# An attention and mixture-of-experts layer: second masks and keys on other engines, the first plan ahead of the last x2, four shared half-layers on either side of the pairs

## The chip, the cores and the metric

The kernel runs on one core of a Trainium2 chip. The metric is the time of one execution on the device, in microseconds (us); the table below also has the span, which is the time from the first to the last recorded instruction. Engines are called by the profile's names too: PE is TensorE (PEld its weight loads), DVE is VectorE, ACT is ScalarE, POOL is GpSimd, SP is SyncE. ACTq and SPq are the DMA issues of these engines.

## What is computed

2048 tokens (two sequences of 1024) of width 128 go through one layer. All of it is float32.

```python
# attention: 8 heads of 16, 2 key-value groups, a window of 32, a sink term in the softmax
mask = (j <= i) & (j > i - WIN)
scores = where(mask, q @ k.T / sqrt(HD), FP16_MIN)
m = max(scores.max(-1), sink_bias)
e = exp(scores - m)
attn = e / (e.sum(-1) + exp(sink_bias - m))
x = layernorm(x + attn @ v @ Wo.T + bo)
# feed-forward: one shared expert for all tokens, and the best 2 of 8 experts for each
shared = (silu(x @ sw1) * (x @ sw2)) @ sw3
w, idx = top_k(softmax(x @ rw + rb), 2)        # w is normalised to a sum of 1
routed = sum of w * ((silu(x @ ew1[e]) * (x @ ew2[e])) @ ew3[e]) over the two experts e
x = layernorm(x + shared + routed)
```

## The kernel before

**Attention.** The tokens are worked off in four chunks of 512 (CHUNKS; `last` is 3), each in four sets of 128 queries. Keys lie in kM (two tiles, used in turn), whose lower 64 partitions hold a mask pattern that is multiplied in with the scores. VectorE writes the masks of both tiles (`spread_masks`, L1043; those of the second at L1448) and the first chunk's keys (L1058); ScalarE writes the keys of the later chunks (`keys`, L846). Per set: scores (PE L581), maximum (DVE L1072), shift (L1079), exp (ACT L872), transposes, weighing of the values (PE L597), `normalise` (DVE L1090 to L1096). Per chunk: `turn` (L1104), the output projection, the sum with x and its statistics (L1106 to L1119), the reciprocal root (POOL L1556), and x2, the normalised rows (DVE L1129; for the last chunk ACT L894).

**Routing.** For every chunk x2 is transposed (PE L619), the router's scores are made (L626), `logits` (DVE L1133) finds the best two experts, `rank` (PE L630) counts places, `gates` and `places` (DVE) give a gate and a row number (pos) for each pick, and `keep_ends` stores how far each expert's list has grown. GpSimd then scatters the chunk's rows into x_list in HBM, eight indirect DMAs of 128 rows each (L1582). The lists are cut into tiles of 128 rows by plans that VectorE works out: the first part (8 tiles) from the counts of chunks 0 and 1 (`plan_full`, `plan_first`), the second (8 tiles) with those of chunk 2, the third (23 tiles) with those of chunk 3. A plan ends with a table (L1219) of row numbers and experts, from which SP, PE, ACT and DVE read registers. `fill_ends` (SP L472) writes eight blocks of blank rows behind the lists' ends; it waits for fill_done, which `keep_ends(last)` gives.

**Experts.** The tiles are taken in 20 pairs (one has a single tile). The iterations of the last stage are numbered by i, and all engines run through them in the same order: iterations 0 to 4 (FIRST_SHARED = 5) are halves of the shared expert's layer for a chunk ("shared half-layers", two for each chunk), 5 to 24 are the pairs, 25 to 27 the last three half-layers. An iteration is: ups (PE L680 and L684, or L694 for a pair), silu (ACT L913, L916), h (DVE L1335, L1339), and, one or two iterations later, downs (PE L711, L725). A pair also needs its rows loaded (SP L483) and turned (PE L667, ACT L907), and its experts' weights copied (DVE L1349, ACT L934). ACT scales its result into y (L925), and POOL scatters y into z_rows in HBM, one indirect DMA for each tile (L1590), 39 in all.

**End.** SP loads z_rows back in five pieces of rows (L488), each when the pairs that can hold its tokens are scattered. VectorE adds shared part and results, makes the statistics, ScalarE and VectorE scale, and SP stores four blocks of rows (L492).

**What sets the order.** Each engine's program is written out by hand and is worked off in order; semaphores tie them together. So POOL never begins with results before the last chunk's scatters, and SP's loads, fills and stores stand in one queue. The order of the steps in iterations 0 to 8 is given by the `if i == ...` lines in the three loops over i (PE L798, ACT L1009, DVE L1498). The names of chunk 2's steps there are written `last - 1`. A few lines of POOL's and SP's programs:

```python
for n in range(CHUNKS - 1):
    scatter(n, 0, 2)
    rstd1_of(n + 1)
    scatter(n, 2)
scatter(last)
for pair in range(ALL_PAIRS):
    scatter_results(pair)
rstd2_of_first()
add_last_results()
```

## Time and profile before

| | |
|---|---|
| time, median of 3 runs | 162.68 us (162.44 to 164.52) |
| time of the profiled execution | 162.66 us |
| its span | 160.6 us |
| busy: PE, DVE, ACT, POOL | 141.4, 117.9, 109.0, 91.1 us |
| mean granted clock of TensorE | 0.979 |

Busy times overlap each other; an engine can be busy for 57% of the span and still be waited for in a part of it. The rows further down are from one profiled execution. A timeline row gives start, length and the instruction with output<-input, and in brackets how long its engine was idle before it and what released it. "issue" there means that it waited for nothing that the profile shows. All starts are counted from the span's start.

### The profile page before, as it was taken

The page shows a single profiled execution, that of the slowest core. Times are in us where ns is not written, and L with a number is a line of the kernel's source. Part 1 is how long each engine was busy: PE and PEld are TensorE (multiplying, and loading weights), DVE is VectorE, ACT ScalarE, POOL GpSimd, SP SyncE. Part 2 cuts the span into 40 slices and gives each one's busy share as a digit, 9 for nine tenths or more (in the row PEclk, how much of TensorE's full clock was granted, in tenths as well). Part 3 has the DMA queues.
Part 4 walks back from the last instruction along what each step waited for, and adds up shares of the span by engine and source line. Part 5 has one row for each costly group of instructions (what it writes and reads, how often), then busy time and mean ns, then how long its engine had stood idle before and what let it go on. Part 6 is the DMA issues. An engine that isn't in the chain of part 4 may idle for free.

```text
span 160.6 us, 3700 instructions
## 1 busy us (share of the span) xinstructions
PE 141.4 (88%) x1078; PEld 119.7 (75%) x1078; DVE 117.9 (73%) x412; ACT 109.0 (68%) x230; POOL 91.1 (57%) x99
## 2 busy tenths in 40 slices
PE   6977978999999889999799999999999999999300
PEld 2166748689959877855479999999999999966300
DVE  6769976998999999999879569234243356786781
ACT  3495999899799986622834567667676676544770
POOL 8723600300284745578777777777776666778430
PEclk9999999999999999999999999999999999999965
DMA  4499960000000110011351753466531191060444
GB/s 83 108 309 379 420 265 6 0 2 0 4 33 33 52 37 17 33 50 50 88 136 50 168 155 99 115 152 171 133 83 49 33 291 52 20 162 10 131 129 132
DMA packets 16962, 17.01 MB, mean 106 GB/s; under 512 B 2555, under 2 KB 15361, under 8 KB 16816
## 3 DMA queue, kind: packets, MB, share of 16 engines
q1 hardware_dynamic: 14304, 12.46, 27.3%
q0 software_dynamic: 2272, 4.24, 8.1%
q8 instruction: 9, 0.15, 0.4%
q10 hardware_dynamic: 368, 0.09, 0.3%
q14 instruction: 9, 0.07, 0.2%
HBM read 10.90 MB, written 6.33 MB: 107 GB/s over the span
## 4 chain that ended last, share of the span: by engine, by line
PE 52%; DVE 18%; ACT 10%; issue 10%; POOL 5%; DMA 2%; ACTq 0%; SPq 0%; DVEq 0%; POOLq 0%
PE att L694 11%; PE gu L694 11%; PE q_bank L725 6%; PE att L725 5%; PE att L581 3%; POOL x_list L1582 3%; PE att L667 3%; ACT probT L884 3%; DMA xT<-x_cols 2%; DVE prob L1079 2%; DVE mx L1072 2%; PE post L626 2%; PE q_bank L556 2%; ACT prob L872 2%; ACT qT L834 2%
## 5 line engine op out<-in xcount | busy, mean ns | idle before, releaser
L1590 POOL DMA_INDIRECT z_rows<-y,xin x39 | 38.9, 996 | 14.1 <-issue 13.5
L1582 POOL DMA_INDIRECT x_list<-x,pos x32 | 31.7, 989 | 25.0 <-DVE x L1162 11.2
L694 PE MATMUL att<-xt,w_pair 128*128 128x128 f32 x160 | 19.6, 275 | 0.0
L694 PEld LDWEIGHTS att<-xt,w_pair 128*128 128x128 f32 x160 | 18.7, 192 | 0.0
L581 PE MATMUL att<-kM,qT 96*128 96x128 f32 x128 | 15.7, 277 | 3.3 <-ACT kM L849 1.6
L694 PE MATMUL gu<-xt,w_pair 128*128 128x128 f32 x152 | 18.6, 275 | 0.0
L597 PEld LDWEIGHTS att<-vbd,probT 128*128 128x128 f32 x128 | 15.4, 191 | 3.4 <-DVE vbd L1065 1.6
L581 PEld LDWEIGHTS att<-kM,qT 96*128 96x128 f32 x128 | 14.8, 192 | 4.0 <-issue 4.0
L694 PEld LDWEIGHTS gu<-xt,w_pair 128*128 128x128 f32 x152 | 17.8, 192 | 0.0
L597 PE MATMUL att<-vbd,probT 128*128 128x128 f32 x128 | 16.8, 280 | 0.5 <-ACT probT L884 0.5
L1339 DVE TENSOR_TENSOR h<-sil,att 128x512 f32<-128x512 f32 x10 | 6.9, 686 | 14.1 <-ACT sil L916 12.2
L1339 DVE TENSOR_TENSOR h<-sil,gu 128x512 f32<-128x512 f32 (+1 forms) x10 | 6.6, 658 | 11.1 <-ACT sil L916 11.1
L872 ACT ACTIVATE prob<-prob 128x512 f32<-128x512 f32 x16 | 10.1, 629 | 4.3 <-DVE prob L1079 4.1
L866 ACT ACTIVATE vT<-gu,bias 32x512 f32<-32x512 f32 x16 | 12.3, 772 | 0.4
L1072 DVE TENSOR_REDUCE mx<-att 128x8 f32<-128x512 f32 x16 | 10.8, 673 | 2.4 <-PE att L581 2.4
L1079 DVE SCALAR_TENSOR_TENSOR prob<-mx,sink,att 128x512 f32<-128x512 f32 x16 | 11.8, 740 | 0.4
L934 ACT ACTIVATE w_pair<-w 128x512 f32 x19 | 11.9, 628 | 0.1
L588 PE MATMUL att<-cst,prob 128*128 128x128 f32 x64 | 9.7, 279 | 1.9 <-ACT prob L872 1.6
L588 PEld LDWEIGHTS att<-cst,prob 128*128 128x128 f32 x64 | 7.2, 140 | 5.5 <-ACT prob L872 4.3
L834 ACT ACTIVATE qT<-q_bank,bias 32x512 f32<-32x512 f32 x15 | 10.2, 679 | 1.2 <-PE q_bank L556 0.9
L916 ACT ACTIVATE sil<-att 128x512 f32<-128x512 f32 x10 | 6.0, 597 | 7.0 <-PE att L694 7.0
L725 PE MATMUL q_bank<-w,h 128*128 x80 | 10.6, 275 | 0.0
(190 smaller groups left out, 305.4 us busy)
## 6 DMA issues: line engine op xcount, KB each, us to landing
w<-weights SPq DMA_DIRECT2D x1, 3456.0 KB, 15.3
xin<-x_list SPq DMA_DIRECT2D x39, 65.0 KB, 2.2
z<-z_rows SPq DMA_DIRECT2D x3, 512.0 KB, 4.6
z_rows<-y,xin POOLq DMA_INDIRECT x39, 2.3
x_list<-blank SPq DMA_DIRECT2D x9, 65.0 KB, 4.0
xT<-x_cols SPq DMA_DIRECT2D x2, 256.0 KB, 3.9
xr<-x_rows SPq DMA_DIRECT2D x2, 256.0 KB, 4.6
xT<-x_cols SPq DMA_DIRECT2D x1, 512.0 KB, 6.6
```

Source lines behind the costliest of these rows:

```text
L581: mm = pe.matmul(att[s][:, j * P:(j + 1) * P], qT[:, s * BPG + j, :, :], kM[n % 2][:, :, at:at + 2 * QB], start=True, stop=True)
L588: mm = pe.transpose(att[s][:, j * P:(j + 1) * P], prob[:, s, j * P:(j + 1) * P], ident)
L597: mm = pe.matmul(att[s][:, j * P:(j + 1) * P], probT[:, s % 2, j * P:(j + 1) * P], vbd[:, at:at + P], start=True, stop=True)
L694: mm = pe.matmul(gu_of(i, q)[:, c * P:(c + 1) * P], w_pair[:, pair % 2, q, c * P:(c + 1) * P], xt[:, pair % 2, q * P:(q + 1) * P], start=T ...
L725: mm = pe.matmul(into[:, q * D:(q + 1) * D], h[:, i % RING, cols], w[:, bass.ds(at[q] + (DOWN + k * D), D)], start=q == 0 and k == 0, stop ...
L834: act.activation(qT[0:GD, :, i, :], blocks(q_bank[rows, :], QB), ACT.Identity, bias=bias[rows, B_Q:B_Q + 1]).then_inc(q_sb, 1)
L872: act.activation(prob[:, s, :], prob[:, s, :], ACT.Exp, scale=-SCALE).then_inc(exp_done, 1)
L1072: dve.tensor_reduce(mx[:, s, :], att[s][:, :].rearrange(by_row, k=2 * QB), AX.X, ALU.max).then_inc(max_done, 1)
L1079: dve.scalar_tensor_tensor(prob[:, s, :].rearrange(by_row, k=2 * QB), mx[:, s, :].unsqueeze(2).to_broadcast([P, BPG * GROUPS, 2 * QB]), si ...
L1339: dve.tensor_tensor(blocks(h[:, i % RING, 0:n * HIDDEN], HIDDEN), blocks(sil[:, i % 2, 0:n * HIDDEN], HIDDEN), blocks(turns[i % 2][:, 0:n ...
L1582: pool.indirect_dma_start(x_list[:, :], bass.IndirectOffsetOnAxis(ap=pos[:, n, k, j:j + 1], axis=0), x2[:, n * ROWT + j, k * ROWW:(k + 1) ...
L1590: pool.indirect_dma_start(z_rows[:, :], bass.IndirectOffsetOnAxis(ap=xin[:, r, q, R_ID:R_ID + 1].bitcast(U32), axis=0), y[:, r, q, :], Non ...
```

## The change

- The masks of the second key tile are written by GpSimd (two copies ahead of its bias sums), and chunk 1's keys by VectorE, between its normalisations of sets 1 and 2 of chunk 0. PE waits for the new semaphore.
- FIRST_SHARED is 4: iterations 0 to 3 are shared, 4 to 23 are the pairs, 24 to 27 are shared.
- On VectorE `plan_first` moves from iteration 1 to 0, and the last chunk's `add_x` and `statistics1` from 0 to 1. The last chunk's transposes, router and rank on PE move from iterations 3, 4 and 4 to 4, 5 and 6 and stand behind the ups there; ScalarE's and VectorE's steps of that chain follow (x2T_out to 5, tanh to 6, logits to 5, gates, places and ends to 6).
- `fill_ends` stands ahead of the loads of pairs 6 and 7 (it stood behind the loads of pair 7).
- y is counted by tile instead of by pair, so that GpSimd can scatter a pair's first tile before the second is scaled.
- Rows of z_rows are numbered so that a piece's load reads one run for each partition.
- At the end the square roots of tiles 8 to 12 come ahead of the first scales, the scales are grouped differently, and the store of tiles 8 to 12 is issued by ScalarE.

The core of the diff:

```diff
-FIRST_SHARED = 5
+FIRST_SHARED = 4
 R_END = FIRST_SHARED + ALL_PAIRS
...
 XRING = 12
+
+PIECES = [(0, 4), (4, 8), (8, 12), (12, 14), (14, 16)]
...
+        def tiles_of(pairs):
+
+            return pairs + second_tiles(pairs)
+
         def tile_weights(eng, engines, pair, q):
...
                 sp.dma_start(z[:, r0:r1, :, :], z_rows[2 * P * r0:2 * P * r1, :]
-                             .rearrange("(t p k) d -> p t k d", p=P, k=2)).then_inc(z_in[piece], 16)
+                             .rearrange("(p t k) d -> p t k d", p=P, k=2)).then_inc(z_in[piece], 16)
...
             for g in range(len(PARTS)):
-                if g == 2:
-                    fill_ends()
                 sp.wait_ge(table_done, g + 1)
...
                 for pair in range(FIRST_PAIR[g], FIRST_PAIR[g + 1]):
+                    if pair == FIRST_PAIR[1] + 2:
+                        fill_ends()
                     load_rows(pair, row)
...
             store_result(0, 8)
-            sp.wait_ge(scaled, 12)
-            store_result(8, 12)
             sp.wait_ge(result_done, 2)
...
                     if n == 1:
-                        pe.wait_ge(masks_done, 5)
+                        pe.wait_ge(later_masks_done, 2)
                     after(pe, k_sb, GROUPS * n)
...
                     pe.wait_ge(base_done, pair + 1)
-                after(pe, y_done, pair - 1)
+                after(pe, y_done, tiles_of(pair - 1) if pair > 1 else 0)
                 into = y_banks[pair % 2]
...
                         rank(last - 1)
-                    if i == 4:
-                        route(last)
                     ups_shared(i, *shared_of(i))
...
                     turn_rows(0)
+                if i == FIRST_SHARED:
+                    transpose_x2(last)
+                if i == FIRST_SHARED + 1:
+                    route(last)
+                if i == FIRST_SHARED + 2:
+                    rank(last)
                 if shared_of(i - 2) is not None:
                     down_shared(i - 2, *shared_of(i - 2))
-                if i == 3:
-                    transpose_x2(last)
-                if i == 4:
-                    rank(last)
                 if pair_of(i - 1) is not None:
...
                 for q in range(width(pair)):
-                    ins = act.activation(y[:, r, q, :], y_banks[pair % 2][:, q * D:(q + 1) * D], ACT.Copy,
-                                         scale=xin[:, r, q, R_GATE:R_GATE + 1])
-                ins.then_inc(y_done, 1)
+                    act.activation(y[:, r, q, :], y_banks[pair % 2][:, q * D:(q + 1) * D], ACT.Copy,
+                                   scale=xin[:, r, q, R_GATE:R_GATE + 1]).then_inc(y_done, 1)
...
             queries(1, 3, HPG)
-            keys(1, 0)
-            keys(1, 1)
             values(1)
...
                     rows_turned(pair_of(i + 1))
-                if i == 4:
+                if i == FIRST_SHARED + 1:
                     x2T_out(last)
+                if i == FIRST_SHARED + 2:
                     router_tanh(last)
...
             act.activation(warm[:, :], eps[:, 0:ROWT], ACT.Sqrt)
+            deviations(8, 12, 3)
             act.wait_ge(first_shift2_done, 1)
-            scale2(0, 4)
-            deviations(8, 12, 3)
-            scale2(4, 8)
+            scale2(0, 8)
             deviations(12, 14, 4)
             act.wait_ge(shift2_done, 1)
-            scale2(8, 10)
+            scale2(8, 9)
             deviations(14, 16, 5)
-            scale2(10, 12)
+            scale2(9, 12)
+            act.wait_ge(scaled, 12)
+            act.dma_start(out[8 * P:12 * P, :].rearrange("(t p) d -> p t d", p=P), total[:, 8:12, :]).then_inc(stored, 16)
...
-            def spread_masks(i):
+            def spread_masks():
                 for at in (GD, GD + QB):
-                    dve.tensor_copy(kM[i][at:at + QB, :, :].rearrange("p g (b k) -> p (g b) k", k=2 * QB),
+                    dve.tensor_copy(kM[0][at:at + QB, :, :].rearrange("p g (b k) -> p (g b) k", k=2 * QB),
                                     pattern[at:at + QB, :].unsqueeze(1)
...
                                       ALU.add).then_inc(q_sb0, 1)
-                dve.wait_ge(kv_mm, 1)
+                keys(0, k_sb0)
+
+            def keys(n, done):
+                dve.wait_ge(kv_mm, n + 1)
                 for g in range(GROUPS):
-                    dve.tensor_scalar(kM[0][0:GD, g, QB:QB + CT], kv_bank[0:GD, :],
+                    dve.tensor_scalar(kM[n][0:GD, g, QB:QB + CT], kv_bank[0:GD, :],
                                       bias[0:GD, B_KVS + g:B_KVS + g + 1], bias[0:GD, B_KVB + g:B_KVB + g + 1],
-                                      ALU.mult, ALU.add).then_inc(k_sb0, 1)
+                                      ALU.mult, ALU.add).then_inc(done, 1)
...
             dve.wait_ge(mask_in, 16)
-            spread_masks(0)
+            spread_masks()
             dve.wait_ge(masks_done, 2)
...
                 softmax_shift(0, s)
-            spread_masks(1)
             dve.wait_ge(place_in, 16)
...
                 normalise(n, 1)
-                if n > 0:
+                if n == 0:
+                    keys(1, k_sb)
+                else:
                     logits(n - 1)
...
                     keep_ends(2)
+                    plan_first()
+                if i == 1:
                     add_x(last)
                     statistics1(last)
-                if i == 1:
-                    plan_first()
                 if i == 2:
...
                 if i == 3:
-                    logits(last)
-                if i == 4:
-                    gates(last)
-                    places(last)
-                    keep_ends(last)
                     add_shared(0)
...
                     add_shared(1)
+                    logits(last)
+                if i == 6:
+                    gates(last)
+                    places(last)
+                    keep_ends(last)
                 if i == 7:
...
+            def spread_later_masks():
+                pool.wait_ge(mask_in, 16)
+                for i in range(2):
+                    at = GD + i * QB
+                    pool.tensor_copy(kM[1][at:at + QB, :, :].rearrange("p g (b k) -> p (g b) k", k=2 * QB),
+                                     pattern[at:at + QB, :].unsqueeze(1)
+                                     .to_broadcast([QB, GROUPS * KW // (2 * QB), 2 * QB])).then_inc(later_masks_done, 1)
+                    pool.wait_ge(later_masks_done, i + 1)
+
             def add_bias(n):
...
                 r = pair % XRING
-                pool.wait_ge(y_done, pair + 1)
                 for q in range(width(pair)):
+                    pool.wait_ge(y_done, tiles_of(pair) + q + 1)
                     pool.indirect_dma_start(
...
             pool.wait_ge(odd_picks_done, 1)
+            spread_later_masks()
             for n in range(CHUNKS):
...
     c[0, C_BASE:C_BASE + EXPERTS] = begin
-    token = np.arange(CHUNKS * ROWT)[None, :, None] * P + row[:, None, None]
-    c[:, C_PLACE:C_PLACE + 2 * CHUNKS * ROWT] = (2 * token + np.arange(2)).reshape(P, -1)
+
+    place = np.zeros((P, CHUNKS * ROWT, 2), np.float32)
+    for r0, r1 in PIECES:
+        place[:, r0:r1] = (2 * P * r0 + 2 * (r1 - r0) * row[:, None, None]
+                           + np.arange(2 * (r1 - r0)).reshape(1, r1 - r0, 2))
+    c[:, C_PLACE:C_PLACE + 2 * CHUNKS * ROWT] = place.reshape(P, -1)
     c[:, C_NOWHERE] = NOWHERE + row
...
     left = np.arange(LEFT)
```

The three places at which the order matters most. First VectorE in iterations 0 to 2, before; `h` rows (L1335) are the ends of iterations, L1109 to L1123 are the last chunk's sum and statistics, L1199 to L1248 the first plan, of which the middle is left out here:

```order
L1181 COPY ends<-post 32x8
L1109 TENSOR_TENSOR res<-att,xr 128x512
L1115 BN_STATS bn<-res 128x6 x4
L1119 BN_AGGR mv<-bn 128x2 x4
L1123 TENSOR_SCALAR lowered<-mv 128x4
L1335 TENSOR_TENSOR h<-sil,att 128x512
L1199 TENSOR_SCALAR passed<-reach,num 32x8
L1201 TENSOR_TENSOR hop<-passed,skip 32x8
```

The same place now (L1204 begins the plan, L1340 is h):

```order
L1250 TENSOR_SCALAR capped<-reach 32x8
L1253 TENSOR_TENSOR since<-capped 32x8
L1340 TENSOR_TENSOR h<-sil,att 128x512
L1114 TENSOR_TENSOR res<-att,xr 128x512
L1120 BN_STATS bn<-res 128x6 x4
L1124 BN_AGGR mv<-bn 128x2 x4
L1128 TENSOR_SCALAR lowered<-mv 128x4
L1340 TENSOR_TENSOR h<-sil,gu 128x512
```

The plan and the second h have moved ahead of the statistics. Next VectorE at the last chunk's places, before: pick and picked are the end of logits, the next h is that of the last shared iteration ahead of the pairs, and pos follows it:

```order
L1151 TENSOR_TENSOR pick<-cst,topi 128x64
L1156 TENSOR_TENSOR picked<-pick 128x32
L1335 TENSOR_TENSOR h<-sil,gu 128x512
L432 TENSOR_LOAD table
L1349 ISA
L1349 COPY w_pair<-w 128x512
L1162 TENSOR_SCALAR x<-half 128x4 x2
L1168 TENSOR_TENSOR placed<-pick,post 128x64
L1173 TENSOR_REDUCE pos<-placed 128x8
L1180 CAST table<-post 1x8
```

The same place now; here the h is that of iteration 6, the third pair (L1344 instead of L1340):

```order
L1156 TENSOR_TENSOR pick<-cst,topi 128x64
L1161 TENSOR_TENSOR picked<-pick 128x32
L1344 TENSOR_TENSOR h<-sil,gu 128x512
L439 TENSOR_LOAD table
L1354 ISA
L1354 COPY w_pair<-w 128x512
L1167 TENSOR_SCALAR x<-half 128x4 x2
L1173 TENSOR_TENSOR placed<-pick,post 128x64
L1178 TENSOR_REDUCE pos<-placed 128x8
L1185 CAST table<-post 1x8
```

The chain up to pos reads the same, but it now ends in iteration 6. Last PE from the last free down to the first pair, before; the transposes (L619) and the router (L626) stand ahead of the pairs:

```order
L711 MATMUL q_bank<-w,h 128x128 x4
L619 MATMUL post<-cst,x 128x128 x4
L680 MATMUL gu<-x2T,w 128x512
L626 MATMUL post<-pw,x2T 128x128 x4
L684 MATMUL gu<-x2T,w 128x512
L654 TENSOR_LOAD table
L667 MATMUL att<-cst,xin 128x128 x2
```

And now, where the transposes (L622) follow the first pair's ups (L697) and the router (L629) the second's:

```order
L714 MATMUL q_bank<-w,h 128x128 x4
L657 TENSOR_LOAD table
L670 MATMUL att<-cst,xin 128x128 x2
L697 MATMUL gu<-xt,w_pair 128x128 x8
L622 MATMUL post<-cst,x 128x128 x4
L714 MATMUL att<-w,h 128x128 x4
L657 TENSOR_LOAD table
L670 MATMUL att<-cst,xin 128x128 x2
L697 MATMUL att<-xt,w_pair 128x128 x8
L629 MATMUL post<-pw,x2T 128x128 x4
```

One shared half-layer has gone from there to the end, and the last chunk's routing has gone in between the pairs.

## Rows read from the trace of the kernel before

**Rows 1.** The page's part 4, shares of the chain that ended last, by engine.

```profile
PE 52%; DVE 18%; ACT 10%; issue 10%; POOL 5%; DMA 2%; ACTq 0%; SPq 0%; DVEq 0%; POOLq 0%
```

**Rows 2.** Timeline of POOL, last chunk's scatters and results; columns: start, length, instruction [idle before].

```profile
84.78 0.96 POOL L1582 DMA_INDIRECT x_list<-x,pos  x1 [0.51 <-DVE pos L1173]
...
95.06 1.00 POOL L1590 DMA_INDIRECT z_rows<-y,xin  x1 [0.30 <-issue]
...
119.75 0.98 POOL L1590 DMA_INDIRECT z_rows<-y,xin  x1 [0.30 <-issue]
...
146.72 0.98 POOL L1590 DMA_INDIRECT z_rows<-y,xin  x1 [0.30 <-issue]
```

**Rows 3.** The tail: timelines of SP and DVE, and the loads of z by tile.

```profile
149.17 0.87 SPq L488 DMA_DIRECT2D z<-z_rows  x2
...
DMA to landing us min/median/max: 2.9/3.9/5.6
...
152.55 0.42 DVE L1362 TENSOR_TENSOR acc<-base,z 128x256 f32<-128x256 f32 x1
...
156.74 1.49 SPq L492 DMA_DIRECT2D out<-total  x3
```

**Rows 4.** Timeline from the start to chunk 1's first maximum.

```profile
5.63 1.44 POOL L1629 COPY qT<-cst 32x1024 f32<-32x1024 f32 x1
...
8.16 1.52 DVE L1058 TENSOR_SCALAR kM<-gu,bias 32x512 f32<-32x512 f32 x2 [0.17 <-PE gu L564]
...
17.33 2.64 DVE L1045 COPY kM<-pattern 32x1152 f32<-32x1152 f32 x2
...
19.93 1.07 PE L564 MATMUL gu<-xT,pw 128*64 128x512 f32 x2
...
22.20 0.16 DVE L1090 SCALAR_TENSOR_TENSOR den<-esink,att 128x8 f32<-128x8 f32 x1 [0.48 <-PE att L597]
...
23.88 0.71 DVE L1104 STREAM_TRANSPOSE oT<-o 128x512 f32<-128x512 f32 x1
...
24.61 2.02 PE L581 MATMUL att<-kM,qT 96*128 96x128 f32 x16 [1.60 <-ACT kM L849]
...
25.78 0.69 DVE L1072 TENSOR_REDUCE mx<-att 128x8 f32<-128x512 f32 x1 [1.18 <-PE att L581]
```

**Rows 5.** Timeline of the routing stage: statistics, plan, x2, loads, pos, fills.

```profile
73.21 0.38 DVE L1119 BATCH_NORM_AGGREGATE mv<-bn 128x2 f32<-128x6 f32 x4
...
74.35 0.22 DVE L1199 TENSOR_SCALAR passed<-reach,num 32x8 f32<-32x8 f32 x1
...
76.28 2.08 ACT L894 ACTIVATE x<-res,shift,rstd 128x256 f32<-128x256 f32 x4 [1.87 <-POOL shift L1561]
...
84.17 0.22 DVE L1173 TENSOR_REDUCE pos<-placed 128x8 uint32<-128x64 f32 x1
...
92.04 4.97 SPq L475 DMA_DIRECT2D x_list<-blank  x8
```

**Rows 6.** Timeline and chain: the first pair's ups, their silu, and the pieces of an iteration.

```profile
84.06 2.01 PE L694 MATMUL att<-xt,w_pair 128*128 128x128 f32 x16
...
86.10 0.60 ACT L916 ACTIVATE sil<-att 128x512 f32<-128x512 f32 x1 [1.46 <-PE att L694]
...
86.07 0.89 PE att L711 x8
86.96 0.22 PE att L667 x2
87.18 1.79 PE gu L694 x16
```

**Rows 7.** Stretches of 1 us at the end: busy time by engine, granted clock, DMA share, GB/s.

```profile
150.00:151.00 1.00, 0.08 (x1) 0.00 (x0) 0.96 (x7) 0.61 (x2) 0.28 (x2) 1.00 0.45 113
...
153.00:154.00 1.00, 0.00 (x0) 0.00 (x0) 0.96 (x2) 0.76 (x2) 0.92 (x2) 0.85 0.00 0
154.00:155.00 1.00, 0.00 (x0) 0.00 (x0) 0.96 (x6) 0.31 (x2) 0.43 (x1) 0.50 0.29 78
```

2 lines of the change are left out of this document (1 added, 1 removed).

## The prediction

> **What bounds the kernel now.** I read first the page's chain of work. It gives PE 52% of the span [rows 1], and it looks as if TensorE set the end all through. The chain is followed back from the last instruction, though, and an engine that is late without being named is found only in its own timeline. So I read GpSimd's timeline next [rows 2]. GpSimd works through one fixed row: for each of the four chunks eight scatters into x_list, then 39 scatters of results into z_rows. The reader is to see three things there. The last chunk's scatters start at 84.78, 0.51 us after GpSimd came free, released by pos: it had just run out of work. From then on it is back to back: eight scatters from 84.78 to 95.06 (10.28 us), and result scatters at a pace of (119.75 - 95.06) / 19 = 1.30 us. At that pace the 38 steps to the last scatter would take 49.4 us, and they take 51.66 (95.06 to 146.72). So its whole slack between pos and the last scatter, time in which it waits for results, is 2.3 us. The last scatter starts at 146.72, and the loads of the last z pieces are issued 2.45 us later, at 149.17. They land 2.9 us after that at the least, and VectorE's last sums start at 152.55 [rows 3]. From there to the end of the span are 8.05 us. So the end hangs on GpSimd's scatters as much as on TensorE, and what starts them is pos of the last chunk.
>
> **The second masks and keys.** VectorE spends 17.33 to 19.97 on the second kM's masks, and then is the last to be ready for chunk 1 [rows 4]. Without them it normalises sets 0 and 1 while TensorE still works. The second K and V projection ends at 19.93 + 1.07 = 21.0. VectorE's two key instructions take as long as the first two, 1.52, so to 22.6. The two last normalisations took 22.20 to 23.88, with a wait in it that is over by then: 1.3, to 23.9. The turn takes 0.71, to 24.6. The first maximum of chunk 1 starts there and not at 25.78, after 1.18 us of idling: 1.2 us gained, and everything behind moves up by it. ScalarE loses its two key instructions, so it isn't late either. The bounds: 1.7 if only TensorE's scores counted, and 0 if GpSimd's two copies disturb the start. They cost about 1.44 x 1152 / 1024 = 1.6 us each, from 7.1 to 10.3, ahead of the bias sums, which wait for a load until 10.9 anyway; beside them stand VectorE's first keys at 8.16. I take 1.2.
>
> The Trainium skill, "SBUF — State Buffer", says on the port pair that VectorE and GpSimd share (section "SBUF: two separate sides") that it is an exclusive lock, held for a whole instruction, so that the loser fully blocks; on VectorE's side it counts fast-mode operations and those with two SBUF inputs. If VectorE's first keys were among them, they would wait out a mask copy of 1.6 us, and the gain of 1.2 would be a loss of 0.4. They have one input, from PSUM, so by the page's own list they aren't. No row here settles it.
>
> **The first plan ahead of the last x2.** All times from here on are on the clock of the profiled execution; the 1.2 comes off at the end. The plan of the first part runs from 74.35, and until then VectorE first did the sum and the statistics of chunk 3, done at 73.21 + 0.38 = 73.59 [rows 5]. Now the plan (1.8) and the second h (0.67) stand ahead of them: 76.1, 2.5 us later. The first table is 2.7 us earlier. GpSimd's reciprocal roots and ScalarE's x2 follow the statistics: x2 runs from 76.28 + 1.5 = 77.8 (it waited 1.87 before, and ScalarE has nothing else meanwhile) to 79.85. Only then come ScalarE's weight copy and the last silu ahead of the pairs (both 128x512, 0.6 by the silu in [rows 6]) and the first turned rows (half as wide, 0.4), to 81.4. So TensorE, with one shared half-layer less ahead, turns the first rows (loaded earlier, with the table) and does its last free down by about 78.2, stands idle and starts the first pair's ups at 81.7 instead of 84.1 [rows 6]. Of the 2.6 us of the moved half-layer some 2.4 are won there.
>
> **Where pos of the last chunk goes.** Before, logits, gates and places of the last chunk are done in iterations 3 and 4, both shared; pos ends at 84.17 + 0.22 = 84.4 [rows 5]. Now the transposes stand behind the ups of iteration 4, the router behind those of 5, rank behind those of 6, and these three are pairs. By the pieces of [rows 6] (ups 1.8, a down 0.9, turned rows 0.2): iteration 4 is ups 81.7 to 83.5, transposes 0.5, down 0.9: 84.9. Iteration 5: rows and ups to 86.9, router 0.9, two downs 1.8: 89.6. Iteration 6: ups from 89.8. Their silu starts 2.0 after them, as in [rows 6], at 91.9, takes 0.6, then h 0.7, a weight copy 0.4, gates 0.25, places and pos 0.45: 94.0. Logits run beside this (from 89.5 to 91.3) and don't add. So pos is 9.6 us later: 94.0, and GpSimd starts at 94.4.
>
> **The sum.** First result scatter: 94.4 + 10.28 = 104.7. At 1.30 each, with results waiting all the way, the last one starts at 104.7 + 49.4 = 154.1, against 146.72: 7.3 later. Loads of z 2.45 later, landing 2.9: 159.4 (before: 152.1, VectorE free at 152.5). Then the tail, 8.05 before. In it SP issues three stores one behind the other, 1.49 us from 156.74 on [rows 3], and the one of tiles 8 to 12 is first. On ScalarE's queue it no longer holds up the two others, which then go out one issue (some 0.45 us) earlier; ScalarE's own store follows its last scale by as much and lands no later. I save 0.45; if ScalarE's store is the last to land, nothing. That z_rows is read in longer runs I count at nothing for its 2.9 (bounds -0.5 and +0.3; it touches no other step), and the counts of y per tile too, since GpSimd is behind by 3 to 10 us all the time and never waits for one. So 159.4 + 7.6 = 167.0; less 1.2 for the attention: 165.8 of span.
>
> To that comes what TensorE does. fill_ends now stands in SP's queue ahead of the loads of pairs 6 and 7, and waits for the last chunk's counts, which come with pos: 94.0. One more us to read the numbers, then the eight fills, 4.97 [rows 5], then the loads: pair 6 is there at about 103, and TensorE wants it at 98.9. Queued behind the fills are all later loads, so TensorE stands still 4 us or more; the loads of pair 8 wait besides for the last chunk's scatters, and come just in time. TensorE then ends at 157.5 and not at 150.1, with the fourth shared half-layer (2.6) behind. VectorE has its shared sums by 158.8, 0.6 ahead of z. That much is cover. But TensorE's granted clock falls when it rests at the end: it comes to rest at 150.1, and the clock is 0.85 in the slice from 153 and 0.50 after it, the lower of its two levels, 1.2 GHz and not 2.4 [rows 7]. The stop ahead of pair 6 may do the same. What work at the lower level costs afterwards no row shows; I set it between 0 and 3 us (one iteration's 2.9 us taking twice as long), less the cover of 0.6. I take a value in the lower half, 0.8, because the clock may also hold. That makes a span of 166.6. The recorded time was 162.66 for a span of 160.6, 2.06 more, and stands at the median (162.68): 168.7 us, 6.0 slower.
>
> **The rivals.** A: the late pos costs nothing, since TensorE alone sets the end, as the page's chain suggests. Then only the 1.2 of the attention and the 0.45 of the stores count: 161.0. For it: PE is busy 88%. Against it: GpSimd has 2.3 us of slack and loses 9.6. It decides from the point at which pos is less than 3.5 us late (the slack and the 1.2); it would take the last chunk's logits to be done during the shared half-layers. B: GpSimd sets the end, but TensorE keeps its clock and z comes in longer runs: 165.8 + 2.06 = 167.9 less up to 0.5, so 167.4. C: the clock falls in the earlier gap too (78.2 to 81.5). Then the iterations ahead of pos run slow, up to 3 us more, and those stand on GpSimd's own path: 168.7 + 2.9 = 171.6. For it: the gap is long; against it: it is shorter than the rest in [rows 7] at the end of which the clock fell. D: the change is faster, since pairs start 2.4 + 1.2 earlier and the fourth half-layer covers the last scatters: 162.7 - 3.6 - 0.45 = 158.6. That was true if pos stayed where it is.
>
> **How the numbers follow.** My forecast (GpSimd late by 6 to 7, some loss on TensorE) 45%; B 22%; C 18%; A 11%; D 4%. A measurement of this kernel can tell about 2%, 3.25 us, from no change. The forecast, B and C are all slower by more; a small part of B (pos at 92 in place of 94) is not. So slower 0.84, same 0.12, faster 0.04. The range takes in B with pos 1.5 earlier (165.3) and C (171.6): 165.0 to 172.0.
>
> **What would show it.** Right: GpSimd idle for 8 us or so ahead of the last chunk's scatters, released by pos near 92.8 (94.0 less 1.2); the first result scatter near 103.5, then no idling to the end; the last z loads issued near 155.3; TensorE idle before the first pair and for 4 us before pair 5's ups, released by an x_list load; chunk 1's first maximum near 24.6. Wrong: a GpSimd that waits for y in the second half, or pos ahead of 88.

## The result, and the profile after

The changed kernel takes 170.78 us (median; 169.99 to 171.34), against 162.67 (162.44 to 164.52) for the kernel before on the same chip: 1.049 times, with an interval of 1.041 to 1.056. It is slower by some 8 us. Ratios and intervals compare fast executions alone: one that is over 1.5% above the fastest of its kernel is left out of them. The profiled execution took 170.56 us, with a span of 168.3 and a mean granted clock of 0.952 (before: 160.6 and 0.979).

The page's chain of work of the changed kernel, shares by engine, as in [rows 1]:

```profile
PE 46%; DVE 25%; issue 10%; ACT 8%; DMA 4%; SPq 3%; POOL 2%; DVEq 0%; ACTq 0%; POOLq 0%
```

It names TensorE first, and GpSimd at 2%, less than before. As before that is one chain of two. GpSimd's timeline, around the last chunk's scatters and at the end, answers to [rows 2]:

```profile
82.92 0.96 POOL L1597 DMA_INDIRECT x_list<-x,pos  x1 [0.30 <-issue]
93.60 0.96 POOL L1597 DMA_INDIRECT x_list<-x,pos  x1 [9.72 <-DVE pos L1178]
...
104.09 1.00 POOL L1605 DMA_INDIRECT z_rows<-y,xin  x1 [0.30 <-issue]
...
153.32 1.12 POOL L1605 DMA_INDIRECT z_rows<-y,xin  x1 [0.30 <-issue]
...
159.93 0.74 POOL L1629 TENSOR_TENSOR acc<-base,z 128x256 f32<-128x256 f32 x1 [3.23 <-DMA z<-z_rows]
```

In brackets stands what the engine waited for. GpSimd is idle for 9.72 us, until pos of the last chunk comes. The first result scatter starts at 104.09 and no longer at 95.06. From there 38 steps in 49.23 us, 1.30 each, without one wait for a result: the last starts 6.6 us later than before.

TensorE's timeline, its two stops and its end (before, the first pair's ups were at 84.06 [rows 6], with no stop in the pairs):

```profile
75.77 0.61 PE L714 MATMUL q_bank<-w,h 128*128 128x128 f32 x4
79.08 0.41 PE L670 MATMUL att<-cst,xin 128*128 128x128 f32 x2 [2.70 <-ACT xt L910]
79.33 2.61 PE L697 MATMUL gu<-xt,w_pair 128*128 128x128 f32 x16
...
102.95 0.69 PE L670 MATMUL att<-cst,xin 128*128 128x128 f32 x2 [4.61 <-DMA xin<-x_list]
103.43 3.62 PE L697 MATMUL att<-xt,w_pair 128*128 128x128 f32 x16
...
156.68 1.95 PE L714 MATMUL att<-w,h 128*128 128x128 f32 x16
```

The pairs start 4.7 us earlier than before, and TensorE ends 8.6 us later (158.63; before 148.03 + 2.05 = 150.08). The ups of a pair take 1.8 to 2.0 us at the full clock. Here the first take 2.61, and those behind the second stop 3.62. The granted clock, in stretches of 1 us (it is the number behind POOL's), shows why:

```profile
80.00:81.00 1.00, 1.00 (x9) 1.00 (x9) 0.97 (x7) 0.00 (x0) 0.70 (x2) 0.78 0.20 67
81.00:82.00 1.00, 1.00 (x7) 1.00 (x7) 0.90 (x7) 0.03 (x1) 0.69 (x2) 0.50 0.12 42
82.00:83.00 1.00, 1.00 (x6) 1.00 (x5) 0.83 (x6) 1.00 (x2) 0.70 (x2) 0.50 0.08 25
...
84.00:85.00 1.00, 1.00 (x11) 1.00 (x10) 0.11 (x1) 0.44 (x2) 0.00 (x0) 1.00 0.20 67
...
101.00:102.00 1.00, 0.00 (x0) 0.00 (x0) 0.29 (x2) 0.00 (x0) 0.70 (x2) 0.52 0.95 204
...
106.00:107.00 1.00, 1.00 (x6) 1.00 (x6) 0.00 (x0) 0.00 (x0) 0.69 (x2) 0.50 0.34 73
...
108.00:109.00 1.00, 1.00 (x11) 1.00 (x10) 0.74 (x2) 0.57 (x3) 0.95 (x1) 1.00 0.75 197
```

It is at 0.50, the lower level (1.2 GHz), behind both stops: some 3 us long behind the first, from 101 to 107.5 around the second. Where TensorE works at that level it is busy all of each microsecond, and does 6 or 7 instructions in it where it does 11 at the full clock.

The timelines of SP and VectorE in the tail, as [rows 3]:

```profile
93.98 4.43 SPq L480 DMA_DIRECT2D x_list<-blank  x8
98.60 11.28 SPq L488 DMA_DIRECT2D xin<-x_list  x13
...
162.66 2.76 SPq L497 DMA_DIRECT2D out<-total  x3
...
159.14 0.66 DVE L1358 TENSOR_TENSOR base<-att,x 128x512 f32<-128x512 f32 x1
...
160.00 0.96 DVE L1367 TENSOR_TENSOR acc<-base,z 128x256 f32<-128x256 f32 x1
```

VectorE's last sums start at 160.00 (before 152.55), 0.07 us behind GpSimd's on the other half of the tiles. VectorE came to them straight from the shared sums, which hung on TensorE's end. GpSimd's had waited for z. So two chains, one through pos and the scatters and one through TensorE's stops, arrive at the end together. The profile alone can't say what either would cost without the other, and the experiments were made for that.

### The profile page after: what moved, and what is told of

The parts are those of the page before. It is cut to its first block, busy times and chain, and to the rows that moved or that the text cites. A ratio compares the mean times of both kernels' runs of the same rounds, so it can differ in the third digit from the quotient of the medians.

```text
span 168.3 us, 3701 instructions
## 1 busy us (share of the span) xinstructions
PE 144.4 (86%) x1078; PEld 123.6 (73%) x1078; DVE 119.0 (71%) x412; ACT 108.0 (64%) x228; POOL 93.0 (55%) x101
## 4 chain that ended last, share of the span: by engine, by line
PE 46%; DVE 25%; issue 10%; ACT 8%; DMA 4%; SPq 3%; POOL 2%; DVEq 0%; ACTq 0%; POOLq 0%
PE att L697 10%; PE gu L697 10%; PE q_bank L728 5%; PE att L728 4%; DVE prob L1084 3%; PE att L670 3%; DVE mx L1077 2%; PE att L600 2%; DMA xin<-x_list 2%; DMA xT<-x_cols 2%; SPq L480 2%; ACT probT L887 2%; PE post L629 2%; DVE kM L1063 2%; PE att L714 1%
## 5 line engine op out<-in xcount | busy, mean ns | idle before, releaser
L1344 DVE TENSOR_TENSOR h<-sil,att 128x512 f32<-128x512 f32 (+1 forms) x10 | 6.6, 661 | 20.7 <-ACT sil L919 20.7
L697 PE MATMUL att<-xt,w_pair 128*128 128x128 f32 x152 | 20.4, 291 | 0.0
L697 PE MATMUL gu<-xt,w_pair 128*128 128x128 f32 x160 | 20.2, 281 | 0.0
L697 PEld LDWEIGHTS att<-xt,w_pair 128*128 128x128 f32 x152 | 19.4, 207 | 0.1
L697 PEld LDWEIGHTS gu<-xt,w_pair 128*128 128x128 f32 x160 | 19.1, 196 | 0.0
L1344 DVE TENSOR_TENSOR h<-sil,gu 128x512 f32<-128x512 f32 x10 | 6.8, 683 | 13.0 <-ACT sil L919 13.0
L670 PE MATMUL att<-cst,xin 128*128 128x128 f32 x39 | 7.9, 284 | 8.3 <-DMA xin<-x_list 5.6
L670 PEld LDWEIGHTS att<-cst,xin 128*128 128x128 f32 x39 | 4.9, 145 | 9.4 <-DMA xin<-x_list 6.6
L910 ACT ACTIVATE xt<-att 128x256 f32<-128x256 f32 (+1 forms) x20 | 7.5, 373 | 5.7 <-PE att L670 5.6
```

Source lines behind the costliest of these rows:

```text
L670: mm = pe.transpose(x_bank[:, i * P:(i + 1) * P], xin[:, r, i, 0:D], ident)
L697: mm = pe.matmul(gu_of(i, q)[:, c * P:(c + 1) * P], w_pair[:, pair % 2, q, c * P:(c + 1) * P], xt[:, pair % 2, q * P:(q + 1) * P], start=T ...
L1344: dve.tensor_tensor(blocks(h[:, i % RING, 0:n * HIDDEN], HIDDEN), blocks(sil[:, i % 2, 0:n * HIDDEN], HIDDEN), blocks(turns[i % 2][:, 0:n ...
```

## The experiments

All times are beside the kernel before on the same chip (162.67 to 162.72 in the three groups). "Five ahead" means FIRST_SHARED = 5.

**1. The fills back behind pair 7.**

```
-                    if pair == FIRST_PAIR[1] + 2:
-                        fill_ends()
+                if g == 2:
+                    fill_ends()
```

> The changed kernel with fill_ends at its old place, behind the loads of pair 7. Theory G (the end hangs on GpSimd, whose row of scatters starts with the late pos of the last chunk): pos near 93, last result scatter near 153.3 as in the changed kernel, time within 0.5 us of its 170.8. Theory T (the end hangs on TensorE, through its stop ahead of pair 6 and the slow clock after it): the stop of 4.8 us goes or moves to pair 8, where it is shorter, and the time falls by 3 us or more.

Measured: 169.85 us (169.27 to 170.86), ratio 1.046 (1.042 to 1.051). Little comes back: 0.9 us, more than the 0.5 that theory G allowed and far from the 3 of theory T. TensorE's stop only moves to pair 8, whose rows wait for the last chunk's scatters:

```profile
107.84 0.69 PE L670 MATMUL att<-cst,xin 128*128 128x128 f32 x2 [3.73 <-DMA xin<-x_list]
...
154.74 1.95 PE L714 MATMUL att<-w,h 128*128 128x128 f32 x16
```

TensorE ends 1.94 us earlier, but GpSimd's sum of the last tiles starts only 0.5 us earlier, at 159.40, and VectorE's waits 0.56 us for z: in this kernel GpSimd's chain is the later one.

**2. Four ahead, but the last chunk's chain and the first plan in the iterations of before.**

```
-                if i == FIRST_SHARED:
+                if i == 3:
                     transpose_x2(last)
-                if i == FIRST_SHARED + 1:
+                if i == 4:
                     route(last)
-                if i == FIRST_SHARED + 2:
+                if i == 4:
                     rank(last)
...
-                if i == 5:
+                if i == 3:
                     logits(last)
-                if i == 6:
+                if i == 4:
                     gates(last)
                     places(last)
                     keep_ends(last)
```

(The route stands ahead of the ups of its iteration, the transposes and rank behind the downs, and ScalarE's x2T_out and router_tanh both in iteration 4, as in the kernel before.)

> The changed kernel (four shared half-layers ahead, masks, keys, tail, fills as changed), but the plan and the last chunk's sum, transposes, router, logits, rank and places in the iterations of the kernel before. Theory G: pos comes back to 85 or 86, the last result scatter to about 146.5, the time to 161 to 163. Theory T, by which moving a half-layer from the front to the back and the fills make the difference: the time stays above 167.

Measured: 168.03 us (167.04 to 169.15), ratio 1.035 (1.030 to 1.041). pos is at 85.09, GpSimd's results start at 96.00, and from 109 on it waits for results. So its chain no longer sets the end, and yet 5 of the 8 us stay: the time is theory T's, and by theory G's numbers (161 to 163) this is a miss. What stays is TensorE's. It ends at 155.2, and VectorE's last sum follows the shared sums without a wait for z:

```profile
77.16 0.44 PE L670 MATMUL att<-cst,xin 128*128 128x128 f32 x2 [2.73 <-DMA xin<-x_list]
...
100.25 0.69 PE L670 MATMUL att<-cst,xin 128*128 128x128 f32 x2 [2.33 <-DMA xin<-x_list]
100.73 3.29 PE L697 MATMUL att<-xt,w_pair 128*128 128x128 f32 x16
...
153.21 1.95 PE L714 MATMUL att<-w,h 128*128 128x128 f32 x16
```

**3. The same with five ahead** (one number changed in experiment 2's kernel).

> As the one before, and five shared half-layers ahead again: what is left of the change is masks, keys, fills, numbering of z_rows, y by tile and the tail. Both theories: faster than before by what attention (1.3) and tail (0.5) bring, 161.0; more than 162.7 would mean that the fills or the numbering cost something.

Measured: 160.59 us (160.32 to 161.35), ratio 0.989 (0.985 to 0.993). One half-layer moved is 7.4 us. From 60 us on TensorE has no stop over 1 us, and it ends at 148.4, against 155.2 in experiment 2. Four ahead starts the pairs only 0.9 us earlier (81.15, here 82.00), since the stops ahead of them (2.73 and 0.96 us, here 0.98) take up the rest of the half-layer's 2.6.

**4. The kernel before with the second masks and keys of the changed one**, nothing else.

> The kernel before with the second masks by GpSimd and chunk 1's keys by VectorE alone. Expected by the prediction's step: 1.2 to 1.3 us less than before, 161.4; the first maximum of chunk 1 earlier by that, counted from chunk 0's first scores. If the gain of the changed kernel's trace (2.0 us at that point) belonged to this edit, 160.7.

Measured: 160.62 us (160.18 to 161.75), ratio 0.990 (0.985 to 0.995). The two engine moves gain about 2 us: 2.1 by the medians, 1.7 by the ratio. They are the whole gain of experiment 3 too: its numbering of z, its stores, its counts of y and its fills add nothing that shows (0.03).

**5. Experiment 2 with the fills behind pair 7.**

```
-                    if pair == FIRST_PAIR[1] + 2:
-                        fill_ends()
...
+                if g == 2:
+                    fill_ends()
```

> The kernel after with four half-layers ahead, but the last chunk's chain and the first plan where they were before, and the fills behind the loads of pair 7. It differs from the run of that kind that measured 168.0 us by the place of the fills alone. Theory F (in that run the fills ahead of pairs 6 and 7 made TensorE's stop at 97 to 100 us, and the stop with its half clock made the loss): the stop goes, the end is at about 159 us, time 161 to 163 us. Theory H (the fourth half-layer is missing as work between the scatters and the pairs, so the row loads come late wherever the fills are): the stop moves to a later pair, as it did for the changed kernel, and the time stays at 166 to 168 us.

Measured: 167.89 us, the median of 164.98, 167.21, 168.58 and 170.45; the ratio, 1.021 with the wide interval 1.010 to 1.031, is that of the two lower ones, 166.1 in the mean. Theory F falls, as its 161 to 163 is far off. Of theory H the mechanism is seen: the stop moves (107.80, 1.71 us, again for a load from x_list), and another stays at 77.88 (2.76). Whether the fills' place gives back nothing or up to 2 us of experiment 2's 168.03 can't be told from executions that differ by 5 us.

**6. Five ahead, with the last chunk's chain as late as in the changed kernel.**

```
-FIRST_SHARED = 4
+FIRST_SHARED = 5
...
-                if i == FIRST_SHARED:
+                if i == 4:
                     transpose_x2(last)
-                if i == FIRST_SHARED + 1:
+                if i == 5:
                     route(last)
-                if i == FIRST_SHARED + 2:
+                if i == 6:
                     rank(last)
```

(The first plan stands behind the last chunk's statistics, as before.)

> The kernel after with five half-layers ahead and the first plan behind x2 as before, but the last chunk's transposes, route, rank, logits, gates and places at the numbers of iterations that the changed kernel gives them. So pos of the last chunk is late (at 90 to 92 us) and GpSimd starts its last scatters late, while TensorE has the work of before ahead of the pairs. Theory G (GpSimd's line of scatters after the late pos sets the end by itself): first result scatter at 101 to 103 us, last one at 151 to 152.5, time 165 to 168 us. Theory T (only TensorE's stops and its lower clock set the end): TensorE doesn't stop, time 160.5 to 163 us.

Measured: 163.48 us (163.42 to 163.94), ratio 1.005 (1.000 to 1.011). pos comes at 87.92 and not at 90 to 92, since with five ahead fewer pairs stand between. TensorE's stops for rows are 1.5 us in sum (two more of 1.1 wait for VectorE's picks and list ends), and it ends at 149.8. GpSimd's chain sets the end:

```profile
88.53 0.95 POOL L1597 DMA_INDIRECT x_list<-x,pos  x1 [5.34 <-DVE pos L1178]
...
148.38 0.98 POOL L1605 DMA_INDIRECT z_rows<-y,xin  x1 [0.31 <-issue]
...
154.16 0.78 POOL L1629 TENSOR_TENSOR acc<-base,z 128x256 f32<-128x256 f32 x1 [2.53 <-DMA z<-z_rows]
```

By both theories' numbers it is a miss. Experiment 3 is the kernel that differs from it by the late chain alone: a start of the scatters 5.6 us later than there (82.97) costs 2.9 us. The sign is theory G's, the size was set for a later pos.

**7. The changed kernel with the first plan behind the last x2.**

```
-                    plan_first()
-                if i == 1:
                     add_x(last)
                     statistics1(last)
+                if i == 1:
+                    plan_first()
```

> The kernel after with the first plan behind the last x2, all else as changed. TensorE's idle stretch from 76.4 to 79.05 us, with its half clock up to 84 us, should be gone or short. Theory G (pos and GpSimd's line bound the end): pos comes at most 1 us earlier, time 169 to 171 us. Theory T (each TensorE gap ahead of the end is paid in full): about 2.5 us of gap and 1.5 us of slow clock come back, time 166 to 167.5 us.

Measured: 169.31 us (168.94 to 170.47), ratio 1.042 (1.035 to 1.048). The first stop doesn't go. It changes its cause, from ScalarE's x2 to the rows themselves, whose table now comes later:

```profile
78.77 0.68 PE L670 MATMUL att<-cst,xin 128*128 128x128 f32 x2 [3.71 <-DMA xin<-x_list]
```

With four half-layers ahead either x2 or the rows are late; the order of plan and x2 only chooses which. The time is theory G's, though pos comes 0.8 us later than in the changed kernel and not up to 1 us earlier.

The time is also 1.5 us below the changed kernel's 170.78. The executions of the two overlap a little (168.94 to 170.47, and 169.99 to 171.34), so the first plan ahead of the last x2 costs some 1 to 1.5 us here, and gains nothing.

Experiments 3, 2, 6 and this one form a square. They have the same fills, masks, keys and tail, and the plan behind:

| | chain early | chain late |
|---|---|---|
| five ahead | 160.59 us | 163.48 us |
| four ahead | 168.03 us | 169.31 us |

The half-layer costs 7.4 us beside the early chain and 5.8 beside the late one; the late chain costs 2.9 us with five ahead and 1.3 with four. So the half-layer is the larger part of the loss, and each covers 1.6 us of the other.

**8. Five ahead, chain and plan early, fills behind pair 7** (experiment 3 with the fills' edit of experiment 5).

> Five half-layers ahead, chain and plan as before, fills behind pair 7: the changed kernel's tail, masks, keys, piece numbering and stores, with nothing of its order of the pairs. Beside the run with the fills ahead of pair 6 (160.59 us) and the run of masks and keys alone (160.62 us). Theory F: the fills' place costs nothing where the pairs' loads have slack: 160.3 to 160.9 us. Rival: the fills forward hid a gain of the tail of 0.4 us or more: 159.6 to 160.2 us.

Measured: 160.22 us (159.98 to 160.36), ratio 0.984 (0.979 to 0.990), the fastest kernel of this study: below the kernel before by 2.5 us and below the changed one by 10.6. Against experiments 3 and 4 it is 0.4 us, between the two expectations and with overlapping intervals; whether the tail or the fills give it is open. Two rows of GpSimd's timeline, the start of the last chunk's scatters and the last result:

```profile
82.97 0.96 POOL L1598 DMA_INDIRECT x_list<-x,pos  x1 [0.30 <-issue]
...
144.67 0.98 POOL L1606 DMA_INDIRECT z_rows<-y,xin  x1 [0.30 <-issue]
```

**9. Experiment 8 with GpSimd held back 10 us by unused powers.**

```
+            for k in range(6):
+                pool.tensor_tensor(delay[:, :], eps[:, :], exponent[:, :], ALU.pow).then_inc(delay_done, 1)
+                pool.wait_ge(delay_done, k + 1)
             scatter(last)
```

> The 160.22 us kernel (five half-layers ahead, early chain, fills behind) with six powers of an otherwise unused 128x8 tile on GpSimd ahead of its last chunk's scatters. A 128x8 power there takes 1.67 us, so the scatters start some 10.4 us later, at about 93.5 us, as they do in the changed kernel (93.60), while TensorE and VectorE have nothing of the change in the order of the pairs. Theory G (the late start of GpSimd's line is enough by itself for the changed kernel's time): first result scatter at 103.5 to 105 us, the last at 152.5 to 154, time 168 to 170.5 us. Theory T (that line has room; TensorE's stops make the loss): time 160.5 to 163 us. If both hold, each alone gives about 168 us and together hardly more, since they end side by side.

Measured: 169.72 us (169.09 to 170.3), ratio 1.042 (1.037 to 1.046).

```profile
83.39 10.26 POOL L1661 TENSOR_TENSOR delay<-eps,exponent 128x8 f32<-128x8 f32 x6
93.94 1.57 POOL L1600 DMA_INDIRECT x_list<-x,pos  x1 [0.29 <-POOL delay L1661]
...
154.68 0.98 POOL L1608 DMA_INDIRECT z_rows<-y,xin  x1 [0.30 <-issue]
...
159.85 0.42 DVE L1370 TENSOR_TENSOR acc<-base,z 128x256 f32<-128x256 f32 x1 [2.23 <-DMA z<-z_rows]
...
109.00 0.69 PE L672 MATMUL att<-cst,xin 128*128 128x128 f32 x2 [5.10 <-DMA xin<-x_list]
```

The last chunk's scatters start at 93.94 and not at 82.97: 11.0 us later (10.3 by the powers, and 0.7 because pos came later in this execution), and the kernel is 9.5 us longer by the medians. So a late start of GpSimd's line is by itself enough for the changed kernel's time. The last row shows a second thing. The late scatters also make the rows of pair 8 late, and TensorE stops 5.10 us for them. It isn't what ends last: TensorE is done at 156.05, and VectorE still waits 2.23 us for z.

**10. Experiment 2 with TensorE's stop ahead of pair 6 filled with matmuls of zeros.**

```
+                if pair == 6:
+                    for _ in range(9):
+                        pe.matmul(x_bank[:, :], idle[:, 0:P], idle[:, :], start=True, stop=True)
                 pe.wait_ge(xin_in[r], 16 * uses(r, pair + XRING))
```

(The wait for ScalarE's xt_sb now stands ahead of the one for xin_in, for every pair.)

> The kernel that measured 168.03 us (four ahead, early chain, fills ahead of pair 6), with nine 128x512 matmuls of zeros in TensorE's 2.3 us stop ahead of pair 6, into the bank that the turned rows then fill. The stop for the rows stays, only the engine isn't idle in it. Theory K (the lower granted clock after a stop costs time by itself): granted clock 1.0 from 100 to 103 us, the ups of pair 5 take 1.8 us where they took 3.1, and 1.2 to 1.8 us come back: 166.3 to 166.9 us. Rival (what the slow stretch costs is made up before the end): 167.7 to 168.4 us.

Measured: 169.42 us (168.74 to 170.97), ratio 1.043 (1.036 to 1.050), where 168.03 had been measured without. In place, theory K's reading holds: the granted clock stays at 1.00 from 97 to 105, and the ups behind the stop take 2.02 us, not 3.29. (The trace has eight of the nine matmuls in one row.)

```profile
100.68 1.89 PE L667 MATMUL att<-idle 128*128 128x512 bf16 x8
102.79 0.44 PE L673 MATMUL att<-cst,xin 128*128 128x128 f32 x2 [0.22 <-DMA xin<-x_list]
103.10 2.02 PE L700 MATMUL att<-xt,w_pair 128*128 128x128 f32 x16
```

Yet the whole is a miss. In this profile the clock had fallen behind the earlier stop, the one at 77 us, which the edit doesn't touch, and in experiment 2's it had not. The same stretch of experiment 10 and then of experiment 2:

```profile
80.00:84.00 4.00, 3.04 (x15) 2.76 (x14) 0.57 (x6) 0.87 (x2) 1.92 (x2) 0.50 0.17 55
```

```profile
80.00:84.00 4.00, 3.85 (x39) 3.84 (x40) 1.94 (x17) 1.17 (x4) 1.92 (x2) 1.00 0.19 58
```

15 instructions on TensorE against 39. That slow stretch lies ahead of pos, and GpSimd's last scatters start at 88.42 and not at 85.71, 2.7 us later. What the filling gives to the whole time can't be told from these two kernels.

**11. Experiment 8 with VectorE's casts later**, one profiled execution.

```
                 if n == 0:
                     keys(1, k_sb)
+                    dve.tensor_copy(bits[:, 0:P], cst[:, C_TRI:C_TRI + P]).then_inc(bits_done, 1)
+                    dve.tensor_copy(bits[:, 2 * P:], cst[:, C_BASE:C_BASE + EXPERTS]).then_inc(bits_done, 1)
```

(The two casts are gone from their old place, ahead of `blank`.)

> The 160.22 us kernel with VectorE's two casts to bf16 of 128x128 and 128x8 behind the keys of chunk 1, at about 21.5 us, when GpSimd's adds of the bias (16.3 to 18.8 us) are over. Theory L (the casts took 1.2 us each because GpSimd worked beside them): 0.15 to 0.25 us each there. Rival (they are slow for their place behind a transfer or for their source): 1.1 to 1.3 us each there too. Time within 0.5 us of 160.2 either way, since the casts were done before the values of chunk 0 were turned.

Measured: 160.84 us, casts of 0.20 and 0.15. It doesn't separate the theories, as the expectation assumed slow casts in experiment 8, and there they took 0.22 and 0.17, ahead of GpSimd's sums. The traces together do: see the last section.

**12. Experiment 8 with six ahead.**

> The 160.22 us kernel with six half-layers ahead of the pairs and two behind. If the fifth half-layer only covers the stops, a sixth covers nothing more and moves the pairs 2.9 us later: the last result scatter at 144 to 146 us instead of 142, the end by GpSimd and the z loads, 161 to 163.5 us. If TensorE's work behind the pairs bounds the end whatever the order, 159.5 to 160.5 us.

Measured: 163.43 us (162.6 to 163.57), ratio 1.003 (1.001 to 1.005). The last result scatter starts at 147.14, and in experiment 8 at 144.67 (the 142 of the expectation was wrong). VectorE waits for z. So five is the better number on both sides. The sixth half-layer leaves the first result scatter nearly where it was (93.71, and 93.09 in experiment 8) but delays the last by 2.5 us, and at four the rows are late.

## Why the prediction was right

It forecast 168.7 us, slower by GpSimd's late start, in a range of 165.0 to 172.0; measured 170.78. Step by step:

- **GpSimd's scatters start with pos and set the end.** Right, and shown. pos was forecast at 92.8 and came at 92.99 + 0.22, the scatters at 93.6, the last result scatter at 152.9 and measured 153.32. Experiment 9 makes the late start alone and gives 169.72; experiment 6 makes half of it and costs 2.9 us. The slack of 2.3 us between pos and the last scatter was right too: in experiment 6 the first result scatter is 5.65 us later than in experiment 3 and the last one 3.35, and in experiment 9 they are 12.0 and 10.0 later than in experiment 8.
- **That pos came so close is in part luck.** The last chunk's statistics ended at 73.86, where 76.1 less 1.2, 74.9, had been forecast, since this execution was ahead by more than the change gives it (see the attention, below). From there to the end of pos it took 19.35 us and not 17.9: the slow clock behind the first stop, which the forecast left out of this path. The two errors nearly cancel. The terms of pos in the prediction also add up to 94.3 and not 94.0. And x2 does follow the statistics by 1.0 us less than before, as forecast, but not because ScalarE had waited: before, GpSimd had first to finish a scatter (from 73.64 to 74.60), and now it was idle for 1.65 us.
- **TensorE's part.** Here the sum was short. The stop ahead of pair 6 was there (4.61 us; 4 or more forecast) and so was the one ahead of the first pair (2.70 us). But the prediction gave the clock 0.8 us and counted it behind the second stop alone. It fell behind both: that is rival C's condition. The first pair's ups were slower by 0.6 us and a down took 1.72 where it takes 0.9; the ups behind the second stop were 1.8 slower. TensorE ended at 158.63 and not at 156.3, and the cover of 0.6 us was used up. Rival C's 171.6 was still too much, for pos came hardly later: the first pair's ups started at 79.3 where 80.5 was forecast, and the slow stretch used that up.
- **TensorE as a second bound.** The prediction held it to be 0.6 us ahead of GpSimd's chain at the end. Experiment 2 shows what that means: with pos early the kernel still takes 168.03. The two losses, 7.4 us by the missing half-layer (experiments 3 and 2) and 9.5 by a GpSimd as late as in the changed kernel (experiment 9), don't add up: the changed kernel loses 10.2. The prediction told the loss as GpSimd's, and didn't say that the moved half-layer would cost nearly as much without it.
- **The attention, 1.2 us.** Right in the profile, rather too small in the times. Chunk 1's first maximum came at 23.78 and not at 25.78, though 0.73 of these 2.0 us are not the change's: the first projection took 1.28 us in one profile and 1.99 in the other. That leaves 1.3, as forecast. It holds in the other traces: from the start of chunk 1's query projection (15.74 before, 15.01 in the changed kernel, 15.13 in experiment 4, 15.27 in 3 and 8) to the first maximum it is 10.04 us before and 8.77 in the four others. Over several executions the edit alone gives 2.1 us by the medians and 1.7 by the ratio (experiment 4), with an interval from 0.8 to 2.5, and experiments 3 and 8 give as much. So 1.3 isn't excluded, and where more would come from is open. GpSimd's copies took 1.17 us each and not 1.6, which touched nothing.
- **The tail, 7.6 us.** It took 8.3. The 0.45 us of the stores don't show: ScalarE's store is issued at 164.79 and SP's last one at 165.0, and the last packets of both leave within 0.1 us of each other, at 167.4. That was the bound at nothing. And VectorE's sum, 0.42 us in experiment 8, takes 0.96 as GpSimd's starts 0.07 us before it. Experiment 8's tail, counted from VectorE's sum, is 8.3 us too, as VectorE waits 0.61 us there for GpSimd's sum, so the tail gained nothing in either kernel.
- **The 2.1 us that the sum is short.** In the profiled execution the last scatter is 0.4 us late (153.32 for 152.9). From it to VectorE's sums are 6.7 us, where 2.45 + 2.9 had been counted and 0.8 for the clock: 0.5, the cost of TensorE's late end. The tail is 0.7 longer. The time is 2.26 us above the span and not 2.06, and the median 0.2 above this execution. So the step that was sized too small is what TensorE's two stops and the clock behind them cost, together with the tail; the mechanism was as forecast. The lower end of the range was worked out wrongly as well: B with pos 1.5 earlier is 167.4 - 1.5 = 165.9 and not 165.3, which changes nothing here.
- **Rivals A and D.** A is excluded by experiments 6 and 9: a late pos costs time from a few us on. Of D the prediction said that it was true if pos stayed where it is. That fails: with pos early and four ahead (experiment 2) the kernel is slower all the same, as the pairs that start earlier run out of rows.

In sum, the order of the pairs costs 10.2 us (170.78 against the 160.59 of experiment 3): 8.7 by the half-layer and the late chain (experiment 7's 169.31), and some 1.5 by the first plan's place. The masks and keys give 2.1 back, and 8.1 are lost.

## What to carry to other kernels

Work that fills the wait for a gather isn't free to move behind it: one half-layer of 2.6 us moved from ahead of the pairs to behind them cost 7.4 us, in stops and in the slow clock behind them. Look for the engine that works through a fixed line at an even pace without idling; what releases its line can set the end, whatever the chain of waits names (here GpSimd stood in it with 2%), and a test that delays that engine alone gives its price directly. Where two chains end within 0.1 us, undo each alone and both together before judging either: with the late chain and the plan's place undone (experiment 2) only 2.7 of the 10.2 us came back.

## What the runs showed of the hardware

**The clock behind a short stop is not settled.** Stops of 2.7 us at 74 to 77 us, in kernels whose code is the same up to there, left a granted clock of 1.00 in one profile and 0.50 in another (experiments 2 and 10, above), and that moved pos by 2.7 us. In experiment 5, whose code is also the same up to there, it was 0.50 behind a stop of 2.76 us, and pos came at 87.41. Counted over the traces of the changed kernel and experiments 1 to 12 from 60 us on: of eleven stops of 2.3 to 5.1 us ten left the clock at 0.50 for some microseconds, one didn't, and behind those of 1.7 and 1.2 us it stayed at 1.00. What the slow stretch cost beyond the stop itself was 1.3 us on the ups of experiment 2, 1.8 on those of the changed kernel, and the 2.7 of pos in experiment 10. Whether stops make the time less repeatable isn't shown. Over four executions the spread is 2.1, 5.5 and 2.2 us in experiments 2, 5 and 10, but 1.2 to 1.6 in experiments 1, 7, 9 and the changed kernel, which stop as long, and 0.4, 1.0 and 1.6 in experiments 8, 3 and 4, which don't.

**VectorE's casts wait for GpSimd.** VectorE's timeline of the changed kernel, the two casts, and GpSimd's sums of the bias beside them:

```profile
16.49 1.18 DVE L1454 CAST bits<-cst 128x128 bf16<-128x128 f32 x1
17.59 1.27 DVE L1455 CAST bits<-cst 128x8 bf16<-128x8 f32 x1
...
16.31 2.52 POOL L1582 TENSOR_TENSOR xr<-xr,cst 128x512 f32<-128x512 f32 x2 [2.55 <-DMA xr<-x_rows]
```

and in experiment 2, where the casts came first:

```profile
16.67 0.22 DVE L1455 CAST bits<-cst 128x128 bf16<-128x128 f32 x1
16.81 0.16 DVE L1456 CAST bits<-cst 128x8 bf16<-128x8 f32 x1
...
16.82 2.53 POOL L1583 TENSOR_TENSOR xr<-xr,cst 128x512 f32<-128x512 f32 x2 [2.77 <-DMA xr<-x_rows]
16.88 0.14 DVE L1457 CAST blank<-cst 128x1 uint32<-128x1 f32 x1
16.95 1.22 DVE L1460 CAST x<-cst 128x32 uint32<-128x32 f32 x1
```

GpSimd's two sums take 1.26 us each. A cast that starts within one ends as that sum ends (17.67 for 17.57, 18.86 for 18.83), and 128x8 takes as long as 128x128. In every profile of this study a cast of 8 columns or more that starts within one of these sums ends within 0.1 us of it, also the 128x32 to uint32 above (18.17 for 18.08). The one of a single column does not: in experiment 2 it starts at 16.88, 0.06 us behind GpSimd's sum, and takes 0.14. Why is open. In experiment 4 the first cast starts ahead of GpSimd and takes 0.22, the second 0.1 us behind it and takes 1.25. The Trainium skill, "SBUF — State Buffer", section "Who interferes with whom", counts copies and casts among the operations that can take the shared port pair; the traces agree. It says too that a VectorE operation with at most one SBUF input, outside the modes that use both port pairs, doesn't contend. The prediction had left that open for the keys, and the trace agrees: with GpSimd's mask copies beside them from 7.14 to 9.48, VectorE's first keys, read from PSUM, took 1.52 us in both kernels [rows 4].

```profile
7.41 1.52 DVE L1063 TENSOR_SCALAR kM<-gu,bias 32x512 f32<-32x512 f32 x2
...
7.14 2.34 POOL L1573 COPY kM<-pattern 32x1152 f32<-32x1152 f32 x2
```
